# DLRM tower with two interaction layers: x transposed as a list of 60 rows, two dimensions at a time, stored once, and triples made by overlapping loads

## The reference, cut to what matters

```python
e = jnp.stack([tbl_0[ids[:, 0]], ..., tbl_38[ids[:, 38]]], axis=1)     # (2048, 39, 16)
z0 = jnp.einsum('bid,bjd->bdij', x0, x0).reshape(B, D, F0 * F0)        # 39 * 39 products
cur0 = jax.nn.relu(jnp.einsum('bdk,kl->bld', z0, W0))                  # W0 (1521, 128)
next_h, direct0 = jnp.split(cur0, 2, axis=1)                           # 64 and 64
z1 = jnp.einsum('bid,bjd->bdij', x0, next_h).reshape(B, D, F0 * Fk)    # 39 * 64 products
cur1 = jax.nn.relu(jnp.einsum('bdk,kl->bld', z1, W1))                  # W1 (2496, 128)
z = jnp.sum(jnp.concatenate([direct0, cur1], axis=1), axis=-1)
h = jnp.concatenate([z, dense_ctx], axis=1)
h = jnp.maximum(h @ W_top1 + b_top1, 0.0)
h = jnp.maximum(h @ W_top2 + b_top2, 0.0)
y = h @ W_top3
```

## Time and profile before

| | |
|---|---|
| median of 3 runs | 1535.93 us |
| lowest and highest | 1534.05 and 1537.34 us |
| the profiled execution's own time | 1532.73 us |
| its span | 1530.9 us |
| busy share of the span: PE, DVE, ACT, POOL | 95%, 90%, 55%, 65% |
| chain that ended last, by engine | PE 83%, POOL 9%, issue 3%, DVE 3%, DMA 1% |
| mean granted TensorE clock | 0.996 of full speed |

### The profile page before, as it was taken

How to read it: one execution, slowest core, us unless ns; L and a number is a source line. 1 busy time by engine, 2 the same in 40 slices (tenths; PEclk the granted TensorE clock), 3 DMA queues, 4 the chain that set the end, 5 groups by cost and what they waited for, 6 DMA issues and landing times.

```text
span 1530.9 us, 15059 instructions
## 1 busy us (share of the span) xinstructions
PE 1448.7 (95%) x4496; PEld 790.7 (52%) x4496; DVE 1374.5 (90%) x1277; ACT 841.2 (55%) x865; POOL 993.5 (65%) x628
## 2 busy tenths in 40 slices
PE   0289999999999999999999999999999999999999
PEld 0144455555555555555555555555555555555565
DVE  0168899999999999999999999999999999999981
ACT  0156555556566555566565555566566555565554
POOL 6788888888888867878587877878587870000000
PEclk9989999999999999999999999999999999999999
DMA  3498978888989888888888888889888887887600
GB/s 88 99 228 214 230 188 214 208 208 206 222 206 213 203 210 211 207 209 204 218 205 217 205 209 208 205 206 211 219 205 205 210 215 203 203 203 195 172 0 1
DMA packets 124578, 294.06 MB, mean 192 GB/s; under 512 B 38016, under 2 KB 48144, under 8 KB 124368
## 3 DMA queue, kind: packets, MB, share of 16 engines
q1 hardware_dynamic: 98000, 264.62, 69.9%
q10 hardware_dynamic: 6528, 23.33, 4.6%
q0 software_dynamic: 19968, 5.15, 3.2%
HBM read 269.61 MB, written 23.34 MB: 191 GB/s over the span
## 4 chain that ended last, share of the span: by engine, by line
PE 83%; POOL 9%; issue 3%; DVE 3%; DMA 1%; ACT 0%; DVEq 0%; ACTq 0%
PE psB L372 39%; PE psA L372 12%; POOL emb L352 9%; PE psB L390 6%; PE psB L397 6%; PE psB L393 6%; PE psA L380 2%; PE psB L380 2%; PE psA L393 2%; PE psA L390 2%; PE psA L397 2%; PE psA L364 2%; DVE z_lo L664 1%; DVE z L656 1%; DVE z_split L656 1%
## 5 line engine op out<-in xcount | busy, mean ns | idle before, releaser
L352 POOL DMA_INDIRECT emb<-in_tbl,ids_all x624 | 993.3, 1592 | 264.3 <-issue 187.1
L372 PE MATMUL psB<-z,w 128*128 128x512 f32 x1536 | 690.5, 596 | 3.6 <-DVE z L656 3.6
L553 ACT ACTIVATE z_hi<-z_split 128x1024 fp32r<-128x1024 f32 x288 | 305.0, 1059 | 486.5 <-DVE z_split L656 441.9
L372 PEld LDWEIGHTS psB<-z,w 128*128 128x128 f32 x1536 | 289.2, 190 | 367.6 <-issue 329.1
L656 DVE TENSOR_TENSOR z<-h_quad,x_lay 128x1024 f32<-128x1024 f32 x352 | 417.5, 1216 | 15.5 <-PE psB L372 8.7
L664 DVE TENSOR_TENSOR z_lo<-z_split,z_hi 128x1024 fp32r<-128x1024 f32 x288 | 351.6, 1221 | 2.3 <-ACT z_hi L553 2.3
L656 DVE TENSOR_TENSOR z_split<-h_quad,x_lay 128x1024 f32<-128x1024 f32 x224 | 270.9, 1221 | 1.3 <-DMA x_lay<-x_rows 1.3
L533 ACT ACTIVATE h_quad<-psA 32x1024 f32<-32x1024 f32 x256 | 259.5, 1014 | 3.8
L372 PE MATMUL psA<-z,w 128*128 128x512 f32 x512 | 244.1, 600 | 9.5 <-DVE z L656 9.5
L390 PE MATMUL psB<-z_hi,w_hi 128*128 128x512 f32 x448 | 158.3, 434 | 0.0
L372 PEld LDWEIGHTS psA<-z,w 128*128 128x128 f32 x512 | 97.7, 192 | 109.3 <-issue 103.4
(11 more groups left out here) (61 smaller groups left out, 847.2 us busy)
## 6 DMA issues: line engine op xcount, KB each, us to landing
x_lay<-x_rows SPq DMA_DIRECT2D x1152, 128.0 KB, 5.9
x_more<-x_rows SPq DMA_DIRECT2D x64, 512.0 KB, 6.7
bases<-x_rows SPq DMA_DIRECT2D x64, 468.0 KB
x_rows<-x_ring ACTq DMA_DIRECT2D x32, 512.0 KB
x_lay<-x_rows SPq DMA_DIRECT2D x64, 256.0 KB, 4.0
emb<-in_tbl,ids_all POOLq DMA_INDIRECT x624
x_last<-x_rows SPq DMA_DIRECT2D x64, 128.0 KB, 6.9
x_rows<-x_ring ACTq DMA_DIRECT2D x32, 200.0 KB
```

The source lines that it names most:

```text
L352: nc.gpsimd.indirect_dma_start(emb[t % 2][:, f * D:(f + 1) * D], None, tables[f], bass.IndirectOffsetOnAxis(ids_all[:, t, f:f + 1], 0)).th ...
L372: mm = nc.tensor.matmul(ps[:, cs], w, z[WHOLE_NO[place] % NZ][0:k, cs], start=first, stop=last)
L553: nc.scalar.activation(z_hi[n % NS][0:k, :], z_split[n % NS][0:k, :], ACT.Copy).then_inc(z_hi_made, 1)
```

## The change

x is no longer spread into triples on the chip. `emb_spread` now holds a plain list of 60 rows a dimension (fields 0 to 38, then 0 to 20 again), copied by two ACT instructions (39 and 21 fields, 8 dimensions each); `wrap` is gone. PE transposes two dimensions at once, 4 transposes a unit, each giving 120 rows. ACT copies 120 rows of 512 floats to a new buffer `x_side`, and two DMAs store them as 60 rows of 1024 floats, in pieces of 128 floats. The triples arise when they are loaded: the access pattern `[[C, rows // 3], [C, 3], [1, C]]` reads rows f, f + 1, f + 2 for every f. The operands of layer 0's six full steps have 126 rows instead of 128. `x_ring` is no longer written by ACT but loaded by SP as `more[0]` (one more DMA a unit, `load_more(u, 0)`), with a semaphore of its own; DVE's first product of a unit waits for it instead of for `x_kept`. The tables for W0 on the host follow the new rows. The steps, their order, and their split into whole and split steps stay.

The diff, cut to its core:

```diff
-WRAP = 6
-RING = SH * 59 + 1
+RING = 60
+ROWS = 3 * (P // 3)
+PAIRS = DH // 2
...
+def shape_of(place):
+
+    half = place in HALF_AT
+    return ROWS if place in RING_AT else P, BANK if half else C
...
+        x_side = sb("x_side", [2 * RING, BANK])
...
-        emb = [sb_loop(f"emb{n}", [P, (F + WRAP) * D]) for n in range(2)]
-        emb_spread = sb_loop("emb_spread", [P, DH, SH * (P // SH + 1)])
+        emb = [sb_loop(f"emb{n}", [P, F * D]) for n in range(2)]
+        emb_spread = sb_loop("emb_spread", [P, DH, RING])
...
+            def ring(u, first, rows):
+                x = x_rows[u, first:first + rows // SH, :]
+                return bass.AP(x.tensor, x.offset, [[C, rows // SH], [C, SH], [1, C]])
+
             def load_base(u, c):
                 if u >= 1:
                     sp.wait_ge(z_made, at0(u - 1, 4 + c) + 1)
-                first = SH * TURNED[c]
-                src = x_rows[u, first:first + ROWS0:SH, :].unsqueeze(1).to_broadcast([F, SH, C])
+                src = x_rows[u, TURNED[c]:TURNED[c] + F, :].unsqueeze(1).to_broadcast([F, SH, C])
                 sp.dma_start(base[c][0:ROWS0, :], src).then_inc(base_loaded[c], 16)
-                sp.dma_start(base[c][ROWS0:P, :], x_rows[u, EXTRA[c]:EXTRA[c] + P - ROWS0, :]).then_inc(base_loaded[c], 16)
+                sp.dma_start(base[c][ROWS0:ROWS, :], ring(u, EXTRA[c] // SH, ROWS - ROWS0)).then_inc(base_loaded[c], 16)
 
             def load_more(u, t):
                 if u >= 1:
                     sp.wait_ge(z_made, at0(u - 1, 2 * t + 1) + 1)
-                sp.dma_start(more[t], x_rows[u, 3 * SH * t:3 * SH * t + P, :]).then_inc(more_loaded[t - 1], 16)
+                sp.dma_start(more[t][0:ROWS, :], ring(u, SH * t, ROWS)).then_inc(more_loaded[t], 16)
...
                 if more_follow:
                     sp.wait_ge(x_stored, 32 * (u + 2) + 32)
                     load_base(u + 2, 0)
+                    load_more(u + 2, 0)
                     load_more(u + 2, 1)
...
-                for d in range(DH):
-                    last = nc.tensor.transpose(half(psA, u)[:, d * P:(d + 1) * P], emb_spread[:, d, 0:P], ident[:, :])
+                for q in range(PAIRS):
+                    pair = emb_spread[:, 2 * q:2 * q + 2, :].rearrange("p d g -> p (d g)")
+                    last = nc.tensor.transpose(half(psA, u)[0:2 * RING, q * P:(q + 1) * P], pair, ident[:, :])
                 last.then_inc(x_turned, 1)
...
-            def wrap(t):
+            def spread_x(u):
+
+                t = u // 2
                 act.wait_ge(gathered[t % 2], 16 * F * (t // 2) + 16 * F)
-                nc.scalar.activation(emb[t % 2][:, F * D:], emb[t % 2][:, 0:WRAP * D], ACT.Copy).then_inc(wrapped, 1)
...
+                for g, count in ((0, F), (F, RING - F)):
+                    src = emb[t % 2][:, 0:count * D].rearrange("p (g d) -> p d g", d=D)[:, DH * (u % 2):DH * (u % 2) + DH, :]
+                    op = nc.scalar.activation(emb_spread[:, :, g:g + count], src, ACT.Copy)
+                op.then_inc(spread, 1)
...
                     act.wait_ge(x_stored, 32 * u)
-                    act.wait_ge(z_made, at0(u - 1, 1) + 1)
-                nc.scalar.activation(x_ring[:, :], half(psA, u), ACT.Copy).then_inc(x_kept, 1)
+                nc.scalar.activation(x_side[:, :], half(psA, u)[0:2 * RING, 0:BANK], ACT.Copy).then_inc(x_kept, 1)
                 act.wait_ge(x_kept, u + 1)
-                act.dma_start(x_rows[u, 0:P, :], x_ring[:, :]).then_inc(x_stored, 16)
-                act.dma_start(x_rows[u, P:RING, :], x_ring[P - ROWS0:RING - ROWS0, :]).then_inc(x_stored, 16)
+                for n in range(2):
+                    dst = x_rows[u, :, :].rearrange("g (q n b) -> n g q b", n=2, b=P)[n]
+                    src = x_side[n * RING:(n + 1) * RING, :].rearrange("g (q b) -> g q b", b=P)
+                    act.dma_start(dst, src).then_inc(x_stored, 16)
...
                 c, t = PRODUCTS0[s]
-                if s == 0:
-                    dve.wait_ge(x_kept, u + 1)
                 if t == 0:
                     dve.wait_ge(base_loaded[c], 32 * u + 32)
-                elif c == 0:
-                    dve.wait_ge(more_loaded[t - 1], 16 * u + 16)
-                make(at0(u, s), C, base[c], more[t])
+                if c == 0:
+                    dve.wait_ge(more_loaded[t], 16 * u + 16)
+                make(at0(u, s), base[c], more[t])
```

72 lines of the change are left out of this document (35 added, 37 removed).

## The result

| | before | changed |
|---|---|---|
| median, first comparison (14 runs each) | 1535.9 us | 1532.24 us |
| ratio, 95% interval | | 0.9973 [0.9962, 0.9984] |
| second comparison, another chip (20 and 5 runs) | 1536.62 us | 1529.87 us |
| ratio, 95% interval | | 0.9959 [0.9945, 0.9973] |
| profiled execution's own time (first) | 1532.73 us | 1532.66 us |

The change is faster, by 4 to 7 us in the medians. The forecast was 10.4 us. The direction was right and so was the bound of most of the program, PE; the size was not. The two profiled executions of the first comparison differ by 0.07 us only, so they are compared place by place, and a second pair of traces (0.9959) is read beside them.

What follows compares the result with a forecast made beforehand. PE was taken as the bound, with DVE less than 2% behind. 11.0 us gained in the regular part and 0.6 us lost at the start gave -10.4 us, 1525.5 us against the median, range 1520 to 1530.

Steps and rivals of the forecast that it cites:

- The bound and the direction: Regular part: PE is the bound, DVE less than 2% behind, no load waited for; faster with chance 0.73.
- PE, the regular part: Transposes of units 4 to 31: four instead of eight save 0.39 us a unit, 11.0 us in all.
- DVE: Regular part: DVE's instructions keep their time; of its 0.80 us spare a unit, 0.41 us is left.
- The rival on DVE: Regular part: DVE becomes the bound, only half of PE's saving fits, gain 5.5 us, time 1531; chance 0.10.
- The start: Units 0 to 2, before 189 us: shorter path against one more load each; 0.6 us lost in the end.
- Absorption by the gathers: Gather wait at 189 us: PE arrives 1.2 us late, slack there absorbs part, 0.6 us stays lost.
- ACT: Spread 0.77 us for 1.13, copy 0.59 for 1.02; worth nothing in the regular part, part of 3.05 us at the start.
- the start eats the gain: Rival: small stored pieces take turns with loads, start costs some 8 to 9 us, -2 us, 1534; chance 0.13.
- The rival on the DMA engines: Uneven spread makes the fullest DMA engine the bound from 0.067 us a stored piece; slower, 1556 to 1649; chance 0.11.

Runs made afterwards that it cites:

- g1: Changed kernel with the copy and store of unit 1's x ahead of ACT's first rounding copy instead of behind it; 1531.57 us, ratio 0.9975.
- g3: Changed kernel with `x_ring` loaded in unit 0 only, so the other units multiply by unit 0's rows; 1528.39 us, ratio 0.9946.
- g2: Changed kernel with x stored in pieces of 512 floats (2 KB) instead of 128, dimensions in another order; 1530.64 us, ratio 0.9961.
- f2: The changed kernel again, unaltered, on a chip without the long stretch of idle engines; 1529.87 us, ratio 0.9959.
- f1: The kernel before, unaltered, run again on a chip without the long stretch of idle engines; 1536.28 us, ratio 0.9999.
- c3: Kernel before with four of eight transposes, their columns copied twice, loads and stores as before, on a chip with the stretch; 1583.82 us.
- g4: Changed kernel with only unit 2's turn and loads moved to earlier places; 1532.16 us, ratio 0.9971.
- h2: Changed kernel with layer 0's full-step operands each loaded by one DMA of 128 rows (other rows than needed), on a chip with the stretch; 1587.58 us.

## Why the prediction was wrong, step by step

- **The bound and the direction: right in the main.** PE is shown busy without a gap from 191 us on, and no load is waited for there. But over three units of four DVE is now as long as PE.
- **PE, the regular part: the turn right, its worth over-counted.** 0.36 us for four transposes was expected as 0.40. But "28 x 0.39 = 11.0 us gained" took every unit to be PE's. The third in a row with sums is DVE's as soon as 0.12 us are saved. 28 x 0.30 = 8.4 us is what came; 2.6 us of the error are here.
- **DVE: the step that failed in the regular part.** DVE "has 0.80 us to spare: 0.41 us is left" is a mean over four unlike units. By the windows its time not busy before was 0.44, 0.10, 2.67 and 0.44 us, and it waited for PE in three of the four: 0.3, none, 2.7 and 0.3 us. The 2.7 us come behind the three units with sums and can't be used in them. The rival on DVE named it ("a mean") and was held too small, because PE had not waited over the sums before; that said nothing on what would happen with each unit 0.40 us shorter. The rival had half of PE's saving lost; 2.6 of 11.0 us, a quarter, were.
- **The start: the step that failed most.** The working has the first products of units 0, 1 and 2 at -0.5, 0.0 and +2.0 us; they came at +1.7, +6.3 and +10.1. "+0.5" for unit 1 set the price of the load against a store that would come 2 us sooner. It came later: the store of unit 1 released SP at 88.68 us, where it had been 85.50. And g1 showed that the regain would have been worth nothing: with the store 8 us sooner the product stands where it stood, while the DMA share is 0.99 up to it. And the delays of units 1 and 2 add up, since unit 2's loads wait for unit 1's `x_lay`; the working counted unit 2's as +2.0 beside a unit 1 that was nearly on time. g3 shows what the reload is: some 3 us at unit 1 and 7 to 8 us at unit 2.
- **Absorption by the gathers: the mechanism right, its size a matter of the execution.** The lateness of 10.1 us at unit 2 is 7.8 us at unit 4 in the first pair of traces, and 9.2 is 3.3 us in the second, since the gathers of before end 3.6 us apart there. The forecast left 0.6 us of 1.2; it was 3.3 to 7.8 of 9 to 10, and which of the two an execution gets, the forecast could not know.
- **ACT: one term mis-sized, one left out.** The spread took 1.10 us where 0.77 was worked out, the copy 0.60 for 0.59. The two stores took 2.32 us to issue at the start and 1.75 later (0.34 + 0.60 before); that was left out of the sum. The first load of unit 0 came 7.0 us behind the end of its gathers (61.77 - 54.76), where it had been 8.7 us (62.70 - 54.04): 1.65 us are gained, and 3.05 were expected. The gathers had ended 0.7 us later in this execution. The load of `x_ring` cost 2.7 us there, for an expected 2.5.
- **The rival "the start eats the gain": near in size, wrong in mechanism.** It had 8 to 9 us lost, by the small pieces. In g2, without the small pieces, and in g1, with an early store, nothing of it came back (1530.64 and 1531.57 us). **The rival on the DMA engines did not come:** a stored piece took 0.030 us, less than half of its threshold. Its sum doesn't hold as a bound either. A row of 4 KB took 0.279 us in the change (78.0% of 16 x 1530.8 us over 280.08 MB), so the count gives 148 x 0.279 + 32 x 0.030 + 1.5 = 43.8 us for the fullest engine, and units of 42.94 us waited for no load. So either the fullest engine pays less than the mean price of a row or the count of its rows is off, and the threshold says little. The Trainium skill, "DMA: Bandwidth & Descriptors", section "Why a DMA increments its semaphore by 16 and not by 1", was the base of that count of engines; q10's 16320 packets are 32 x 510, that is 480 pieces and 2 x 15 closing packets, as the rule has it for 60 rows.

Sum of what was measured: -8.4 in the regular part and +7.8 or +3.3 up to unit 4 (the shorter turns of units 2 and 3 are in that) give -0.6 and -5.1 us. The own times of those two pairs differ by -0.07 and -3.45, the medians by -3.7 and -6.7, where executions of one kernel lie some 4 to 7 us apart. What the second pair lacks is behind the last turn, unit 31's: from there to the end are 170.2 us in f2 and 168.5 in f1, as in both traces of the first pair (168.6). In f2 the granted clock is 0.57 of full speed from 1474 to 1478 us, after PE had stood 2.12 us, and it is 1.00 in f1 from 1475 to 1495.

Still open: what the even spread would save at unit 1 on a chip without the stretch; whether the engines' lower rate in the change's variants (209 GB/s at 0.99 in g1 against 242 at 0.93 in f1) comes from the spread, the overlapping rows or the number of packets; why the stretch of 64 us exists on some chips, and why the kernel before loses some 17 us more there than the changed one (1610.9 - 1536.3 against 1588.8 - 1531), while with four transposes it doesn't (c3, 1583.8 against 1527.1); no trace of the kernel before was taken on such a chip.

## What to carry to other kernels

Read the spare time of the second engine unit by unit over a whole cycle, not as a mean, and add up its work over the units in which it has no pause: a saving of 0.4 us a unit was cut to 0.3, because DVE's work over three units of four was as long as what PE would have needed, and its pause came only in the fourth. A load added to every unit cost no wait in the regular part here and had its full price at the start, where each unit waits for its own loads, and there the prices add up from unit to unit until something else, here the gathers, is later. Issuing the store or the loads sooner did not help where the DMA share was 0.99 (g1), and moving loads forward in one queue moved the wait to the loads behind them (g4).

## What the runs showed that was not expected

- A load of 9 rows, three by three, took 0.78 us to issue and one of 126 rows 0.82 to 0.84, where 128 plain rows had taken 0.36 and 11 plain rows 0.52. 128 rows read as 32 x 4 took 0.54 to 0.60 (h2). The issue time goes with the pattern more than with the rows.
- Two stores in pieces of 512 B took 1.75 us to issue, the same bytes in pieces of 2 KB 0.78 us (g2).
- The regular part's cover was large: q1's share of the DMA engines rose from 69.9% to 78.0% for 6% more bytes, and no load was waited for in the regular part.
- The stretch on some chips: PE, DVE and ACT idle from 90 to 140 us, the granted clock at 0.50, the lower of its two levels, from 100 us on, after PE had stood still since 86 us, and POOL gathering on at its own pace.
